# A static order by lag and list, and a static order by one turn number per piece, for a fused attention and recurrence kernel

## The chip, the cores and the metric

The kernel runs on one core of a Trainium2 chip. The core has five engines that run side by side, each through its own list of instructions in the order in which the list was written: TensorE (PE, matmuls), VectorE (DVE), ScalarE (ACT), GpSimd (POOL) and SyncE (SP, which here issues every DMA). An instruction may wait for semaphores; what stands behind it on the same engine waits with it. The metric is the time of one execution in microseconds. Timed runs of the kernel before gave a median of 693.77 us (3 runs, 692.63 to 694.01).

## The reference

For each of 16 sequences of 128 tokens with 256 channels, in float32:

```
# block L0, on x[b] and the context ctx[b]
x = x + attention(layernorm(x), mask of the first kind) @ w_ao      # 16 heads of 16
x = x + attention(layernorm(x), keys and values from ctx, mask[b]) @ w_co
x = x + gelu(layernorm(x) @ w1) @ w2                                # 4 * 256 hidden
# block L1, a recurrence over the 128 tokens, with first states from ctx[b]
xn = layernorm(x); five mixed streams of xn and its shifted difference
w = exp(-exp(decay)); r, k, v, g = projections of the streams       # 32 heads of 8
s_t = k_t v_t + w_t s_(t-1);  out_t = r_t (u k_t v_t + s_(t-1))
x = x + (groupnorm(out) * silu(g)) @ Wo
x = x + sigmoid(xr @ Wr) * (square(relu(xk @ Wk)) @ Wv)             # xk, xr mixed as above
```

In the attention, `scores = scores * mask - 10000 * (1 - mask)` comes before the softmax. The sequences do not depend on each other.

## The kernel before, in words

**Pieces.** The work on one sequence b (called item b below) is cut into small functions, "pieces", each with one engine. Their first letter names the stage: `a_` is the attention (second argument 0 for the self attention, 1 for the cross attention; a pair such as `(0, 2)` is the attention and a group of four heads), `b_` is the MLP and the preparation of the recurrence, `d_` is the recurrence and all after it. Each engine has 80 to 1408 pieces in all. Those that matter below:

- `a_scale` on ACT (line 1231, `A_LT<-PS_S`) turns a normalised x, transposed by PE (`a_turn`), into the layer's input. `a_val`, `a_key`, `a_query` on PE wait for it, and the scores wait for those.
- `a_lessmask` on ACT (line 1272, `MADD<-MASK`) makes `10000 * mask[b] - 10000` for the cross attention of item b. For b = 0 it waits for `in_rest`, the semaphore of two DMAs from line 473 (all cross masks) and line 474 (x of items 1 to 15). In later items it does not wait for a DMA.
- `a_exps` on ACT are the exponentials, `a_prob_turn`, `a_pv` and `a_out` on PE the rest of the attention.
- `b_decay2`, `b_decays` on ACT make the decays (`DW` line 1356, `EW` line 1362), which SP spreads over 8 rows with a DMA (`b_wspread`). `b_keyrec` (`KR`, line 1350) and `b_values` (`VC`, line 1370) move keys, receptances and values out of PSUM; PE's `b_valgate` writes into the same PSUM bank that `b_keyrec` of ACT empties and so waits for it. `b_gatetanh` is `TG` (line 1375).
- `d_outer` (AJ), `d_scan` (SS, line 1057) on DVE are the recurrence. In the last two items the values are spread by PE (`b_select`, line 767).
- `d_root_of` on ACT (line 1407, a square root, and for item 14 a short `Tanh` behind it at line 1410) and DVE's `d_inverse`, `d_norm` are the group norm in the last two items; the other items do it with Newton steps on DVE. `d_yturn` (PE, `PS_D<-CST,O`), `d_affine` (ACT, line 1431), `d_gated` (DVE, `YT`), `d_out` (PE, line 559 `PS_D<-W,YT`), `d_sum` (DVE, line 1166) follow each other.
- `b_shift` (SX, line 1520) and `d_shift` (SM, line 1531) on POOL take differences of two SBUF tensors.

**Order.** The order of an engine's list is written out by hand: a table per engine (`PE_ORDER` and so on) with rows (piece, argument, lag). The program goes through steps i = 0, 1, ..., and in each step through the table; the row issues its piece for item i - lag, where such an item exists. So all items have the same order inside a step, those at the start and the end included; up to seven items are in work at once. No piece is left out and none is issued twice. `KEEP_WARM` adds matmuls on the identity in front of some PE pieces of the first and the last items.

**ACT tables.** Some functions of ACT need another table than the one that is loaded (`ACT_TABLE_LOAD` in the list); the compiler puts a load wherever the function that follows asks for another table, so their number depends on the order.

Its wait for the DMAs:

```
def a_lessmask(b, _):
    if not later(b):                       # later(b) is b > 0
        act.wait_ge(in_rest, IN_REST)
```

Of the kernel before, what the change touches and what calls it, by code (L numbers as in the profile page):

```python
# [88 lines left out]
PE_ORDER = [
    ("a_prob_turn", (1, 0), 3), ("d_own", 0, 5), ("a_prob_turn", (1, 1), 3), ("b_low2", 2, 4), ("d_read", 0, 5),  # L90
    ("a_prob_turn", (1, 2), 3), ("b_decay1", 0, 4), ("d_oturn", 0, 5), ("a_enc_turn", 0, 2),
    ("a_prob_turn", (1, 3), 3), ("b_decay2", 0, 4), ("b_keyrec", 0, 4), ("b_keyrec", 1, 4), ("a_val", 1, 2),
    ("a_pv", 1, 3), ("a_turn", 1, 2), ("b_valgate", 0, 4), ("b_valgate", 1, 4), ("a_key", 1, 2), ("a_out", 1, 3),
    ("a_query", 1, 2), ("d_biasout", 0, 5), ("d_yturn", 0, 5), ("a_prob_turn", (0, 0), 1), ("a_scores", 1, 2), ("a_prob_turn", (0, 1), 1),
    ("b_select", 0, 4), ("b_turn", 0, 3), ("d_out", 0, 5), ("a_turn", 0, 0), ("b_mlp1", 0, 3), ("b_mlp1", 1, 3),
    ("b_mlp2", 0, 3), ("a_prob_turn", (0, 2), 1), ("d_turn", 0, 5), ("b_mlp2", 1, 3), ("a_val", 0, 0),
    ("a_key", 0, 0), ("b_select", 1, 4), ("a_prob_turn", (0, 3), 1), ("a_query", 0, 0), ("a_pv", 0, 1),
    ("b_turn", 1, 3), ("d_keyrec", 0, 5), ("d_keyrec", 1, 5), ("a_out", 0, 1), ("b_low1", 0, 3), ("d_val", 0, 5),
    ("a_scores", 0, 0), ("b_low2", 0, 3)]
DVE_ORDER = [  # L100
    ("a_mask", (0, 1), 1), ("b_streams", 0, 4), ("a_prob_copy", (1, 1), 3), ("d_own", 0, 5),
    ("a_addmask", (0, 1), 1), ("b_streams", 1, 4), ("a_inverse", 1, 3), ("b_streams", 2, 4), ("a_maxima", (0, 0), 1),
    ("d_output", 0, 5), ("a_prob_copy", (1, 3), 3), ("d_means", 0, 5), ("d_centre", 0, 5), ("a_mask", (0, 2), 1),
    ("a_normal", 1, 2), ("d_spread", 0, 5), ("d_guess", 0, 5), ("a_mask", (0, 3), 1), ("d_guess", 1, 5),
    ("d_guess", 2, 5), ("a_maxima", (0, 1), 1), ("d_newton", (0, 0), 5), ("d_newton", (0, 1), 5),
    ("d_newton", (0, 2), 5), ("d_newton", (1, 0), 5), ("d_newton", (1, 1), 5), ("a_stats", 0, 0),
    ("d_newton", (1, 2), 5), ("a_moments", 0, 0), ("d_newton", (2, 0), 5), ("a_context", 1, 3),
    ("d_newton", (2, 1), 5), ("a_maxima", (0, 2), 1), ("a_addmask", (0, 3), 1), ("a_key", 1, 2),
    ("d_newton", (2, 2), 5), ("a_normal", 0, 0), ("d_inverse", 0, 5), ("d_norm", 0, 5), ("d_ruk", 0, 4), ("a_sum", 1, 3),
    ("b_stats", 0, 3), ("b_moments", 0, 3), ("a_query", 1, 2), ("a_maxima", (0, 3), 1), ("d_gated", 0, 5),  # L110
    ("b_normal", 0, 3), ("b_gate", 0, 4), ("a_mask", (1, 0), 2), ("a_mask", (1, 1), 2), ("a_mask", (1, 2), 2),
    ("d_sum", 0, 5), ("a_prob_copy", (0, 1), 1), ("a_mask", (1, 3), 2), ("d_stats", 0, 5), ("a_maxima", (1, 0), 2),
    ("a_addmask", (1, 3), 2), ("d_moments", 0, 5), ("a_maxima", (1, 1), 2), ("a_maxima", (1, 2), 2),
    ("d_outer", 0, 4), ("d_normal", 0, 5), ("d_scan", 0, 4), ("b_sum", 0, 3), ("b_stats", 1, 3),
    ("a_prob_copy", (0, 3), 1), ("a_inverse", 0, 1), ("a_key", 0, 0), ("b_moments", 1, 3), ("d_shift", 0, 5), ("d_mixed", 0, 5),
    ("a_maxima", (1, 3), 2), ("b_normal", 1, 3), ("d_rstate", 0, 4), ("d_mixed", 1, 5), ("d_outer", 1, 4),
    ("a_context", 0, 1), ("a_query", 0, 0), ("b_mixed", 0, 3), ("d_scan", 1, 4), ("d_relu2", 0, 5), ("d_mixing", 0, 5), ("d_final", 0, 5), ("a_sum", 0, 1),
    ("a_stats", 1, 1), ("a_mask", (0, 0), 0), ("a_moments", 1, 1), ("d_rstate", 1, 4)]
ACT_ORDER = [
    ("a_exps", (1, 0, 0), 3), ("a_prob_copy", (0, 3), 2), ("a_key", (0, 0), 1), ("a_widen", 0, 2),  # L120
    ("a_exps", (1, 0, 1), 3), ("a_spread", 0, 2), ("b_scale", 1, 4), ("a_exps", (1, 1, 0), 3), ("a_val", 0, 1),
    ("d_keyrec", 0, 6), ("d_relu2", 0, 6), ("a_key", (0, 1), 1), ("b_low", 0, 4), ("a_exps", (1, 1, 1), 3),
    ("a_exps", (1, 2, 0), 3), ("a_exps", (1, 2, 1), 3), ("a_prob_copy", (1, 0), 3), ("d_first_states", 0, 4),
# [11 lines left out]
    ("a_root", 1, 2), ("a_addmask", (0, 2), 1), ("a_addbias", 0, 1), ("a_root", 0, 0), ("a_addbias", 1, 2),  # L135
    ("b_root", 0, 3), ("b_addbias", 0, 3), ("a_addmask", (1, 0), 2), ("a_addmask", (1, 1), 2),
    ("a_addmask", (1, 2), 2), ("d_gates", 0, 5), ("d_root", 0, 5), ("d_shift", 0, 5), ("b_root", 1, 3), ("b_shift", 0, 3),
    ("d_rstate", 0, 4)]

LAG = max(lag for order in (SP_ORDER, PE_ORDER, DVE_ORDER, ACT_ORDER, POOL_ORDER) for _, _, lag in order)  # L140

# [1495 lines left out]
```

## Time and profile before

| what | value |
| --- | --- |
| timed runs, median | 693.77 us |
| profiled execution, span from first to last instruction | 694.0 us |
| PE busy | 645.3 us, 93% |
| DVE busy | 598.2 us, 86% |
| ACT busy | 571.7 us, 82% |
| POOL busy | 311.6 us, 45% |
| DMA | 50.44 MB, mean 73 GB/s |
| chain that ended last | PE 80%, DVE 8%, ACT 7% |

The span of the profiled execution is 0.2 us over the median of the timed runs and inside their spread; there is nothing around the span that has to be added. The page of the profile gives, in 40 slices of 17.35 us, the busy share of each engine in tenths. The views by window give the busy time of each engine in a stretch; the timelines give single instructions with their start, their length, and in brackets how long the engine had been idle and what ended that.

### The profile page before, as it was taken

What the parts mean: (1) busy time and instruction counts of PE and PEld (TensorE: products, weight loads), DVE (VectorE), ACT (ScalarE), POOL (GpSimd) and SP (SyncE); (2) the same over time, 40 slices, a digit from 0 to 9 for tenths busy, and PEclk for the clock granted to TensorE, in tenths of its full rate; (3) what the DMA queues carried; (4) which work ended last, traced back from release to release, by engine and by line L of the source; (5) the groups of instructions that cost most, each with busy time, mean ns of one, the idle gap of its engine ahead of it and who ended that gap; (6) DMA issues with size and microseconds to landing.
All of it is one profiled execution on the core that took longest, in us unless ns stands there. A gap on an engine that the chain in (4) does not pass through costs nothing.

```text
span 694.0 us, 17297 instructions
## 1 busy us (share of the span) xinstructions
PE 645.3 (93%) x5877; PEld 561.6 (81%) x5877; DVE 598.2 (86%) x1430; ACT 571.7 (82%) x2071; POOL 311.6 (45%) x440
## 2 busy tenths in 40 slices
PE   6878998999999999999999999999999989898776
PEld 5666787888989888988989888989888877687555
DVE  3598588999999999999999999999999987968274
ACT  1568899899999999999999999999999987664513
POOL 1154252646464554636364646454554624432120
PEclk9999999999999999999999999999999999999799
DMA  8920031221305050504122231305050503120200
GB/s 306 325 70 9 2 104 36 70 70 58 88 9 138 1 146 1 145 2 122 25 85 62 67 81 53 93 4 144 1 146 1 146 0 108 31 70 0 69 9 8
DMA packets 53725, 50.44 MB, mean 73 GB/s; under 512 B 6030, under 2 KB 48902, under 8 KB 53254
## 3 DMA queue, kind: packets, MB, share of 16 engines
q1 hardware_dynamic: 53638, 49.34, 24.7%
q8 instruction: 47, 0.77, 0.5%
q14 instruction: 40, 0.33, 0.1%
HBM read 28.62 MB, written 3.93 MB: 47 GB/s over the span
## 4 chain that ended last, share of the span: by engine, by line
PE 80%; DVE 8%; ACT 7%; issue 3%; POOL 1%; DMA 0%; SPq 0%; DVEq 0%; ACTq 0%; POOLq 0%
PE PS_B L552 16%; PE PS_T L654 9%; PE PS_B L694 8%; PE PS_S L552 7%; PE PS_D L559 5%; PE PS_S L625 4%; PE PS_T L662 4%; PE PS_S L559 4%; PE PS_T L559 4%; ACT SC L1291 3%; PE PS_D L800 2%; PE PS_B L703 2%; PE PS_D L552 2%; ACT PT L1301 2%; PE PS_T L545 2%
## 5 line engine op out<-in xcount | busy, mean ns | idle before, releaser
L1291 ACT ACTIVATE SC<-SC,NMX 128x128 f32<-128x128 f32 x512 | 200.0, 398 | 0.2
L1291 ACT ACTIVATION_READ_ACCUMULATOR SC<-SC,NMX 128x1 f32 x512 | 101.0, 197 | 0.0
L654 PE MATMUL PS_T<-CST,SC 128*128 128x128 f32 x512 | 81.3, 281 | 7.7 <-ACT PT L1301 3.6
L976 DVE TENSOR_REDUCE NMX<-SC 128x4 f32<-128x512 f32 x128 | 85.2, 676 | 0.4 <-POOL SC L1499 0.3
L1301 ACT ACTIVATE PT<-PS_T 128x512 f32<-128x512 f32 x120 | 70.8, 590 | 12.7 <-PE PS_T L654 12.7
L654 PEld LDWEIGHTS PS_T<-CST,SC 128*128 128x128 f32 x512 | 56.4, 141 | 26.1 <-ACT PT L1301 12.7
L1057 DVE TENSOR_TENSOR_SCAN SS<-W,AJ 128x1024 f32<-128x1024 f32 x32 | 73.2, 2288 | 0.2
L552 PE MATMUL PS_B<-MX,W 128*128 128x128 f32 x512 | 64.2, 280 | 4.7 <-ACT KR L1350 4.7
L552 PEld LDWEIGHTS PS_B<-MX,W 128*128 128x128 f32 x512 | 61.3, 196 | 4.9 <-ACT KR L1350 4.9
L1499 POOL TENSOR_TENSOR SC<-SC,MADD 128x512 f32<-128x512 f32 x48 | 59.9, 1276 | 6.5 <-DVE SC L956 6.5
L552 PE MATMUL PS_B<-B_LT,W 128*128 128x128 f32 x512 | 61.1, 278 | 1.0 <-ACT B_LT L1231 0.9
L694 PE MATMUL PS_B<-W,HG 128*128 128x256 f32 x256 | 61.9, 385 | 0.0
L552 PEld LDWEIGHTS PS_B<-B_LT,W 128*128 128x128 f32 x512 | 58.4, 192 | 3.2 <-ACT B_LT L1231 1.9
L1501 POOL TENSOR_TENSOR SC<-SC,MADD 128x512 f32<-128x512 f32 x32 | 42.2, 1318 | 40.4 <-DVE SC L956 40.4
L956 DVE TENSOR_TENSOR SC<-PS_S,MASK 128x512 f32<-128x512 f32 x80 | 51.9, 683 | 4.0 <-PE PS_S L625 4.0
L552 PE MATMUL PS_S<-A_LT,W 128*128 128x128 f32 x384 | 51.8, 280 | 1.3 <-DVE SC L967 1.3
L552 PEld LDWEIGHTS PS_S<-A_LT,W 128*128 128x128 f32 x384 | 50.3, 196 | 3.1 <-DVE SC L967 1.5
L1544 POOL TENSOR_TENSOR SS<-SS,KR 128x1024 f32<-128x1024 f32 x14 | 33.1, 2363 | 41.0 <-DVE SS L1057 41.0
L694 PEld LDWEIGHTS PS_B<-W,HG 128*128 128x128 f32 x256 | 46.1, 190 | 5.6
L1536 POOL TENSOR_TENSOR MX<-MX,XN 128x256 f32<-128x256 f32 x80 | 48.4, 634 | 3.1 <-DVE MX L1029 2.9
L1262 ACT ACTIVATE KP<-PS_S,KB,CST 128x128 f32<-128x128 f32 x112 | 46.1, 480 | 0.8 <-PE PS_S L552 0.8
L1029 DVE SCALAR_TENSOR_TENSOR MX<-PS_B,COL,SX 128x128 f32<-128x128 f32 x160 | 44.1, 336 | 0.7 <-PE PS_B L716 0.7
(231 smaller groups left out, 1595.0 us busy)
## 6 DMA issues: line engine op xcount, KB each, us to landing
W<-EW SPq DMA_DIRECT2D x32, 512.0 KB, 4.1
...
```

The source lines that it names most:

```text
L552: last = pe.matmul(dst[:, m * T:(m + 1) * T], w(name, kt, n, lo + m * P, lo + (m + 1) * P), rhs[:, kt, 0:T], start=(kt == 0), stop=(kt == ...
L559: last = pe.matmul(dst, lhs[:, kt, 0:T], w(name, kt, n, lo, lo + C), start=(kt == 0), stop=(kt == CT - 1))
L654: last = pe.transpose(PS_T[:, j * T:(j + 1) * T], SC[:, nr(b, a) % 2, g, j, :], ident)
L694: last = pe.matmul(PS_B[:, 1, 0:C], HG[:, kt, :], w("w2", kt, C, 0, C), start=(kt == 0), stop=(kt == FT - 1))
L956: dve.tensor_tensor(masked, PS_S[:, g], over_heads(mask), ALU.mult).then_inc(a_masked, 1)
L976: dve.tensor_reduce(NMX[:, nr(b, a) % 2, GH * g:GH * g + GH], SC[:, nr(b, a) % 2, g], AX_X, ALU.max, negate=True)\
L1057: dve.tensor_tensor_scan(SS[:, t].rearrange("p d n -> p (d n)"), W8[:, t].rearrange("p d n -> p (d n)"), AJ[:, t].rearrange("p d n -> p (d ...
L1262: last = act.activation(KP[:, par, t, :], keys[:, t * T:(t + 1) * T], ACT.Identity, bias=KB[:, a, par, t:t + 1], scale=CST[:, K_PAR + par: ...
L1291: last = act.activation(SC[:, nr(b, a) % 2, g, j, :], SC[:, nr(b, a) % 2, g, j, :], ACT.Exp, bias=NMX[:, nr(b, a) % 2, h:h + 1], accum_out ...
L1301: act.activation(PT[:, g], PS_T[:, :].rearrange("p (j n) -> p j n", n=T), ACT.Copy)\
L1499: pool.tensor_tensor(SC[:, nr(b, a) % 2, g], SC[:, nr(b, a) % 2, g], over_heads(MADD[:, b % 2, :]), ALU.add).then_inc(a_added, 1)
L1536: last = pool.tensor_tensor(MX[:, i], MX[:, i], XN[:, :, 1:T + 1], ALU.add)
```

## The change

Each row of a table now holds a turn number instead of a lag, and a second table per engine (`..._MOVED`) holds other turn numbers for single items. A piece of item b has the place `10000 * b + turn`, and an engine's pieces are issued in the order of these places. The instructions of the pieces, their semaphores and their waits are as before, and so is `KEEP_WARM`. The set of pieces on each engine is the same: 80 on SP, 800 on PE, 1408 on DVE, 944 on ACT, 336 on POOL.

```diff
+TURN = 10000
+
 SP_ORDER = [
-    ("b_vspread", 0, 4), ("d_store", 0, 6), ("b_wspread", 0, 3), ("b_vstore", 0, 3), ("a_load", 0, 0)]
+    ("a_load", 0, 90000), ("b_wspread", 0, 110004), ("b_vstore", 0, 110008), ("b_vspread", 0, 120002),
+    ("d_store", 0, 170026),
+]
...
+ACT_MOVED = {
+    ("a_scale", 0): {0: -49998, 2: 9934, 4: 8789, 12: 7950}, ("a_key", (0, 0)): {4: 10734, 15: 10413},
...
+    ("a_lessmask", 0): {0: -50000, 1: -59996, 5: 17742, 10: 27746, 12: 25187, 13: 22838},
...
+def in_order(order, moved):
+
+    turns = [(TURN * b + moved.get((name, arg), {}).get(b, turn), name, arg, b)
+             for name, arg, turn in order for b in range(B)]
+    return [(name, arg, b) for _, name, arg, b in sorted(turns, key=lambda t: t[0])]
...
-        def run(pieces, order, i):
-
-            for name, arg, lag in order:
-                if 0 <= i - lag < B:
-                    pieces[name](i - lag, arg)
+        def run(pieces, order, moved):
+
+            for name, arg, b in in_order(order, moved):
+                pieces[name](b, arg)
...
-            for i in range(B + LAG):
-                run(pieces, ACT_ORDER, i)
+            run(pieces, ACT_ORDER, ACT_MOVED)
```

The file is 153 lines longer ahead of the pieces, so line 1272 of before is line 1425 of the change, 1231 is 1384, and so on. What moves is shown at three places.

**The first instructions of ACT.** `A_LT` is `a_scale` of item 0, `VP` its `a_val`, `MADD` is `a_lessmask`; in brackets stand the semaphores waited for. Before:

```order
L1224 ACTIVATE EARLY<-EW 128x1 [waits set_dve]
L1231 ACTIVATE A_LT<-PS_S,COL 128x128 [waits a_lnps,set_dve,in_first]
L1231 ACTIVATE A_LT<-PS_S,COL 128x128
L1253 ACTIVATE VP<-PS_S 128x8x16 [waits a_pvps,a_vps]
L1253 ACTIVATE VP<-PS_S 128x8x16
```

The same place in the change:

```order
L1377 ACTIVATE EARLY<-EW 128x1 [waits set_dve]
L1425 ACTIVATE MADD<-MASK 128x128 [waits in_rest,set_dve,in_first]
L1384 ACTIVATE A_LT<-PS_S,COL 128x128 [waits a_lnps]
L1384 ACTIVATE A_LT<-PS_S,COL 128x128
L1425 ACTIVATE MADD<-MASK 128x128
L1406 ACTIVATE VP<-PS_S 128x8x16 [waits a_pvps,a_vps]
```

`a_lessmask` of item 0, with its wait for `in_rest`, now stands ahead of `a_scale` of item 0, and that of item 1 behind it. Before, the one of item 0 was the 23rd piece of ACT.

**ACT in the last two items.** `DW`, `EW`, `KR`, `VC`, `TG` belong to item 15, `OQ`, `GE` and `PS_D<-PS_D,GNC` to the group norm of item 14. Before:

```order
L1356 ACTIVATE DW<-PS_B,COL 128x128 x2
L1401 ACTIVATE OQ<-O 128x256
L1407 ACT_TABLE_LOAD
L1407 ACTIVATE GE<-PS_D,EPST 128x32
L1410 ACT_TABLE_LOAD
L1410 ACTIVATE EARLY<-EW 128x1
L1362 ACTIVATE EW<-DW 128x2x127
L1364 ACT_TABLE_LOAD
L1364 ACTIVATE EARLY<-EW 128x1
L1350 ACTIVATE KR<-PS_B 128x512
L1370 ACTIVATE VC<-PS_B 128x256
L1375 ACT_TABLE_LOAD
```

The same place in the change:

```order
L1509 ACTIVATE DW<-PS_B,COL 128x128 x2
L1515 ACTIVATE EW<-DW 128x2x127
L1517 ACT_TABLE_LOAD
L1517 ACTIVATE EARLY<-EW 128x1
L1503 ACTIVATE KR<-PS_B 128x512
L1560 ACTIVATE GE<-PS_D,EPST 128x32
L1563 ACT_TABLE_LOAD
L1563 ACTIVATE EARLY<-EW 128x1
L1584 ACTIVATE PS_D<-PS_D,GNC 128x128 x2
L1528 ACTIVATE TG<-PS_B 128x256
L1523 ACTIVATE VC<-PS_B 128x256
```

`EW` and `KR` of item 15 now stand ahead of the square root of item 14, and the stretch holds two table loads instead of four.

**PE in the last two items.** `PS_B<-MX,W` are the key, receptance, value and gate matmuls of item 15 (four pieces of four), `PS_D<-CST,O` is `d_yturn`, `PS_D<-W,YT` `d_out` of item 14, `PS_S<-VC,SEL` `b_select` of item 15. Before:

```order
L746 MATMUL PS_B<-DT,W 128x128 x2
L552 MATMUL PS_B<-MX,W 128x128 x16
L545 MATMUL PS_D<-CST,O 128x128 x2
L767 MATMUL PS_S<-VC,SEL 128x128 x8
L541 MATMUL PS_T<-CST 128x128 x2
L559 MATMUL PS_D<-W,YT 128x256 x2
```

The same place in the change:

```order
L901 MATMUL PS_B<-DT,W 128x128 x2
L707 MATMUL PS_B<-MX,W 128x128 x12
L700 MATMUL PS_D<-CST,O 128x128 x2
L707 MATMUL PS_B<-MX,W 128x128 x4
L696 MATMUL PS_T<-CST 128x128 x2
L714 MATMUL PS_D<-W,YT 128x256 x2
L922 MATMUL PS_S<-VC,SEL 128x128 x8
```

`d_yturn` of item 14 went ahead of the last four of the sixteen, and `b_select` of item 15 behind `d_out` of item 14.

## Rows read from the trace of the kernel before

**Rows 1.** The page, 40 slices: busy tenths of PE, then its granted clock.
```profile
PE   6878998999999999999999999999999989898776
PEclk9999999999999999999999999999999999999799
```

**Rows 2.** Busy us by window: window, length, PE, PEld, DVE, ACT, POOL, clock, DMA.
```profile
0.00:40.00 40.00, 28.95 (x205) 23.76 (x205) 21.74 (x55) 15.82 (x63) 10.49 (x19) 1.00 0.88 303
40.00:160.00 120.00, 108.85 (x1027) 93.15 (x1026) 100.33 (x221) 106.56 (x404) 52.19 (x75) 1.00 0.15 42
160.00:560.00 400.00, 398.70 (x3805) 353.00 (x3804) 385.93 (x949) 379.96 (x1395) 211.05 (x291) 1.00 0.26 70
560.00:640.00 80.00, 71.40 (x606) 60.46 (x605) 62.71 (x149) 51.74 (x176) 30.19 (x43) 0.96 0.16 46
640.00:694.00 54.00, 37.44 (x240) 31.21 (x240) 27.48 (x60) 17.63 (x38) 7.72 (x14) 0.87 0.09 27
```

**Rows 3.** Timeline of ACT, first 38 us: start, length, instruction, idle before and its end.
```profile
8.27 0.81 ACT L1231 ACTIVATE A_LT<-PS_S,COL 128x128 f32<-128x128 f32 x2 [6.03 <-PE PS_S L545]
...
32.14 0.32 ACT L1272 ACTIVATE MADD<-MASK 128x128 f32<-128x128 f32 x1
37.30 0.17 ACT L1241 ACTIVATE PREV<-PS_S 128x4 f32<-128x4 f32 x1 [4.83 <-PE PS_S L545]
```

**Rows 4.** Timeline of SP, the DMA of x for items 1 to 15.
```profile
5.74 6.40 SPq L474 DMA_DIRECT2D X<-in_x  x1
```

**Rows 5.** Timeline of DVE, first 36 us: what waited for that DMA.
```profile
21.51 0.43 DVE L890 BATCH_NORM_STATS2 A_ST<-X 128x6 f32<-128x256 f32 x1 [1.02 <-DMA X<-in_x]
```

**Rows 6.** Timeline of PE, first 36 us: the first matmuls on `A_LT`.
```profile
9.13 2.08 PE L559 MATMUL PS_S<-W,A_LT 128*128 128x256 f32 x4
11.00 3.19 PE L552 MATMUL PS_S<-A_LT,W 128*128 128x128 f32 x16
```

**Rows 7.** Timeline of ACT, 645 to 660 us.
```profile
646.24 0.62 ACT L1356 ACTIVATE DW<-PS_B,COL 128x128 f32<-128x128 f32 x2 [0.80 <-PE PS_B L746]
...
647.28 1.28 ACT L1407 ACT_TABLE_LOAD   x1
648.58 0.29 ACT L1407 ACTIVATE GE<-PS_D,EPST 128x32 f32<-128x32 f32 x1
648.88 1.28 ACT L1410 ACT_TABLE_LOAD   x1
650.18 0.20 ACT L1410 ACTIVATE EARLY<-EW 128x1 f32<-128x1 f32 x1
650.29 0.40 ACT L1362 ACTIVATE EW<-DW 128x254 f32<-128x254 f32 x1
...
652.11 0.58 ACT L1350 ACTIVATE KR<-PS_B 128x512 f32<-128x512 f32 x1
...
658.53 0.77 ACT L1431 ACTIVATE PS_D<-PS_D,GNC 128x128 f32<-128x128 f32 x2
```

**Rows 8.** Timeline of PE, 640 to 662 us.
```profile
642.03 1.94 PE L800 MATMUL PS_D<-SS,HS 128*32 128x256 f32 x16
...
652.74 3.78 PE L552 MATMUL PS_B<-MX,W 128*128 128x128 f32 x16 [4.75 <-ACT KR L1350]
...
660.13 1.03 PE L559 MATMUL PS_D<-W,YT 128*128 128x256 f32 x4
```

**Rows 9.** Timeline of DVE, 638 to 694 us.
```profile
649.29 0.42 DVE L1148 TENSOR_TENSOR O<-O,PS_D 128x256 f32<-128x256 f32 x1
...
661.19 0.42 DVE L1166 TENSOR_TENSOR X<-PS_D,X 128x256 f32<-128x256 f32 x1 [0.98 <-PE PS_D L559]
...
663.74 2.29 DVE L1057 TENSOR_TENSOR_SCAN SS<-W,AJ 128x1024 f32<-128x1024 f32 x1
```

**Rows 10.** All instructions of POOL's line 1520: length in ns, least, median, most.
```profile
L1520 POOL TENSOR_TENSOR SX<-XN x16: 612/612/1749, 83.4 to 634.7; 128x256 f32<-128x256 f32 x16
```

**Rows 11.** Timeline of POOL, 584 to 640 us.
```profile
601.64 1.75 POOL L1520 TENSOR_TENSOR SX<-XN 128x256 f32<-128x256 f32 x1 [2.01 <-ACT XN L1231]
```

**Rows 12.** Timeline of DVE, the same stretch.
```profile
601.70 1.22 DVE L1050 TENSOR_TENSOR AJ<-V,KR 128x1016 f32<-128x1016 f32 x1
```

More of the change, by code:

```diff
@@ L84 @@
     ('d_keyrec', 0, 15): 4, ('d_val', 0, 15): 2}
+TURN = 10000
 SP_ORDER = [
-    ("b_vspread", 0, 4), ("d_store", 0, 6), ("b_wspread", 0, 3), ("b_vstore", 0, 3), ("a_load", 0, 0)]
-PE_ORDER = [
[L90 to L99, printed above, removed]
@@ L100 @@
-DVE_ORDER = [
[L101 to L118, printed above, removed]
@@ L133 @@
-POOL_ORDER = [
-    ("d_final", 0, 6), ("a_addmask", (0, 0), 1), ("b_addnorm", 0, 4), ("b_addnorm", 1, 4), ("b_addnorm", 2, 4),
[L135 to L140, printed above, removed]
+    ("a_load", 0, 90000), ("b_wspread", 0, 110004), ("b_vstore", 0, 110008), ("b_vspread", 0, 120002),
@@ new lines @@
+    ("d_store", 0, 170026),
+]
+SP_MOVED = {
+    ("b_wspread", 0): {11: 120002, 12: 110008, 13: 110006}, ("b_vstore", 0): {2: 110002, 11: 120004, 12: 120002},
+    ("b_vspread", 0): {1: 110012, 11: 120006, 12: 120004},
+}
+PE_ORDER = [
+    ("a_turn", 0, 5845), ("a_val", 0, 7312), ("a_key", 0, 7410), ("a_query", 0, 7959), ("a_scores", 0, 9566),
+    ("a_prob_turn", (0, 0), 14631), ("a_prob_turn", (0, 1), 15131), ("a_prob_turn", (0, 2), 16323),
+    ("a_prob_turn", (0, 3), 17781), ("a_pv", 0, 18202), ("a_out", 0, 19031), ("a_enc_turn", 0, 21631),
+    ("a_val", 1, 22442), ("a_turn", 1, 22844), ("a_key", 1, 22853), ("a_query", 1, 24031), ("a_scores", 1, 24831),
+    ("a_prob_turn", (1, 0), 30031), ("a_prob_turn", (1, 1), 30431), ("a_prob_turn", (1, 2), 30972),
+    ("a_prob_turn", (1, 3), 31868), ("a_pv", 1, 32831), ("a_out", 1, 33632), ("b_turn", 0, 35637),
+    ("b_mlp1", 0, 36078), ("b_mlp1", 1, 36150), ("b_mlp2", 0, 36409), ("b_mlp2", 1, 36882), ("b_turn", 1, 38500),
+    ("b_low1", 0, 39300), ("b_low2", 0, 39900), ("b_low2", 2, 40700), ("b_decay1", 0, 41287), ("b_decay2", 0, 42100),
+    ("b_keyrec", 0, 42362), ("b_keyrec", 1, 42500), ("b_valgate", 0, 42974), ("b_valgate", 1, 43267),
+    ("b_select", 0, 45545), ("b_select", 1, 47695), ("d_own", 0, 50300), ("d_read", 0, 50900), ("d_oturn", 0, 51479),
+    ("d_biasout", 0, 54337), ("d_yturn", 0, 54513), ("d_out", 0, 55700), ("d_turn", 0, 56793), ("d_keyrec", 0, 58705),
+    ("d_keyrec", 1, 58900), ("d_val", 0, 59500),
+]
@@ L519, in _ @@
             pieces = named(a_load, b_vstore, b_vspread, b_wspread, d_store)
-            for i in range(B + LAG):
-                run(pieces, SP_ORDER, i)
+            run(pieces, SP_ORDER, SP_MOVED)
             sp.wait_ge(stored, 16 * B)
@@ L864, in _ @@
                            d_own, d_read, d_oturn, d_yturn, d_biasout, d_out, d_turn, d_keyrec, d_val)
-            for i in range(B + LAG):
-                run(pieces, PE_ORDER, i)
+            run(pieces, PE_ORDER, PE_MOVED)
         @block.vector
@@ L1216, in _ @@
                            d_moments, d_mixed, d_mixing)
-            for i in range(B + LAG):
-                run(pieces, DVE_ORDER, i)
+            run(pieces, DVE_ORDER, DVE_MOVED)
         @block.scalar
@@ L1569, in _ @@
                            d_rstate, d_gates, d_root)
-            for i in range(B + LAG):
-                run(pieces, POOL_ORDER, i)
+            run(pieces, POOL_ORDER, POOL_MOVED)
 def kernel(**inputs):
```

183 lines of the change are left out of this document (169 added, 14 removed), and 3 rows, old and new, of the table PE_MOVED.

## Prediction, on record before the change was run

> **What bounds the kernel now.** I read the page first. Its 40 slices [rows 1] show PE at 9 tenths in all slices from the eighth to about the thirty-second, and lower at both ends. The same in windows [rows 2]: from 160 to 560 us PE is busy for 398.70 of 400 us, DVE for 385.93 and ACT for 379.96, at the full granted clock. Here no order can gain more than the 1.3 us in which PE is idle, because the PE instructions are the same. What an order can gain or lose lies at the ends: PE is idle for 11.05 us from 0 to 40, 11.15 us from 40 to 160, 8.60 us from 560 to 640 and 16.56 us from 640 to 694 [rows 2]. So I looked at both ends in the timelines, engine by engine, and held the new order against them. Two places carry nearly the whole sum, and they have opposite signs.
>
> **The start: a wait moved to the head of ACT.** Before, ACT's first work on data is `a_scale` of item 0, which starts at 8.27 us, when PE has turned the normalised x [rows 3]. Everything follows from it: PE's value, key and query matmuls at 9.13 and 11.00 us [rows 6], then the scores, the masks and the exponentials. In the change `a_lessmask` of item 0 stands ahead of it, and it waits for `in_rest`. The second DMA of that semaphore is issued at 5.74 us [rows 4] as the tenth of a row. When it lands is shown by DVE: it sat idle 1.02 us for this very DMA and went on at 21.51 us [rows 5]. ACT does this instruction only at 32.14 us before [rows 3], when the data had long been there, and so pays nothing.
>
> In the change ACT starts it at about 21.5 us. The instruction is 0.32 us long [rows 3]; the next one may start some 0.1 us before its end. So `a_scale` starts at 21.5 + 0.2 = 21.7 us instead of 8.27, which is 13.4 us later. Queued behind it on ACT is everything that ACT does. PE's next piece, `a_val` of item 0, waits for `a_scale`; DVE's next, `a_key` and `a_query` of item 0, wait for PE; POOL's next, the first mask sum, waits for DVE. There is nothing of another item ahead of them on any engine, so nothing hides the 13.4 us. SP goes on with its loads, but none of these is waited for before 13.4 us later except the one here: the 1.02 us that DVE idles for x of item 1 falls away, yet ACT was busy with exponentials then, and I count nothing for it. The `a_lessmask` of item 1 (0.32 us) lies behind `a_scale`, where ACT waits for PE's value matmuls of 2.08 us [rows 6]: nothing. These four records of 2.08 us take 1.03 us at 660.13 [rows 8]: twice as long, so they run at the lower of the clock's two levels (1.2 of 2.4 GHz), although the window's mean reads 1.00. In the change PE has again been idle before them, and I let the same matmuls take the same time. Bounds of this term: below 12.0 us, if the DMA lands earlier by the spread that one landing may have (a tenth of its 15.8 us from issue to the start at 21.51); above 15.5 us, if as much half clock comes again behind these matmuls as they show (2.08 and 3.19 us in [rows 6] are together some 2 us over the full clock). I take 13.4.
>
> **The end: two table loads less.** From 640 us few pieces are left and one chain runs through all engines. Before, between the decays and `KR` of item 15 ACT does the square root of item 14's group norm, with a table load before it and one behind [rows 7]: 1.28 + 0.29 + 1.28 + 0.20, from 647.28 to 650.29, are 3.0 us. PE sits idle 4.75 us for `KR` at the end of it [rows 8]. In the change `EW`, a load and `KR` come first, then the root. With DW ending as before, `KR` starts at 652.11 - 3.0 = 649.1 and ends at 649.7.
>
> From there I follow item 14, since the recurrence of item 15 on DVE stands behind its sum. The root (0.29) is done at 650.0; DVE's reciprocal and `d_norm` (before 0.7 us from the root's end at 648.87 to the end of `O` at 649.71 [rows 7, 9], so 0.8) at 650.8. PE has done the first four value matmuls by then, and `d_yturn` stands right behind them and no longer behind all of 3.78 us [rows 8]: about 651.2. ACT has loaded its table by 650.0 + 1.28 + 0.20 = 651.5, which is later, so `d_affine` starts at 651.5. Before, it started at 658.53 [rows 7]. That is 7.0 us. In front of DW, in the matmuls of item 14's read-out and item 15's streams, the new order puts `d_own`, `d_read` and `d_oturn` together, and the record of 1.94 us in [rows 8] lies in a half-clock stretch; here I estimate 1.5 us, from nothing (no gain) to 3 us (the 1.94 us halved, and `d_oturn` before two matmul groups). What is late next: from `d_affine` the chain goes on over `d_out` and the sum at 661.19 to the scan at 663.74 [rows 8, 9], in the same steps. `b_select` of item 15 is now behind `d_out`, but the scan's first multiplication waits for item 14's sum and its statistics on DVE anyway (661.19 to 662.3), which is about as long as four of the eight matmul pairs. The row of the decays that SP spreads starts 3 us earlier too. Sum of the end: 7.0 + 1.5 = 8.5 us earlier. Bounds: 3.0, if only the path to `KR` shortens and the rest waits for something else; 11, with the 3 us in front and 1 us of the clock.
>
> **Meetings on the shared port.** POOL's line 1520, two SBUF tensors of 256 elements, takes 612 ns in the median and 1749 ns at most [rows 10]. The long one is at 601.64 us, beside DVE's multiplication of two SBUF tensors from 601.70 to 602.92 [rows 11, 12], and DVE waited for it after. The 16 executions have a median equal to the minimum, so in the steady part there is no such meeting in this line to be taken away. I take 1.14 us (1749 - 612) for the one on the path, and bound it by 0 and 2.
>
> The Trainium skill (SBUF — State Buffer, section "SBUF: two separate sides") says that VectorE, with two SBUF inputs, and GpSimd take an exclusive lock on a shared port pair for the whole instruction and that the loser is fully blocked. The trace agrees: the two instructions of rows 11 and 12 show 1749 against 612 ns. By this rule the change's numbers could also make new meetings wherever they shift one list against the other, and then the term would be zero or a loss; that it would be a gain in the steady part the rule does not give, with no meeting in line 1520 there.
>
> **The start after the first waits (40 to 160 us).** The PE idle of 11.15 us is made of many waits below 1.5 us; ACT has the longest, 4.83 us, at 37.30 [rows 3]. In the change the query and scores of item 1 stand ahead of item 0's `a_out`, which brings item 1's exponentials forward and item 0's cross attention back. My value is 1.0 us gained. The trace doesn't show the new order, so the bounds are wide: a gain of half the idle time, 5.6 us, or a loss of 2 us. The orders of the stores on SP cost nothing: nobody waits for `d_store` but the end, and the last one is last in both.
>
> **The sum.** Against the profiled execution's span: 694.0 + 13.4 - 8.5 - 1.1 - 1.0 = 696.8 us. The span is 0.2 us over the median of the timed runs, nothing is added around it, and I forecast 697.
>
> **Rivals.**
>
> 1. *The ends give back more than the start costs* (faster). Half of the idle time from 40 to 160 us, 5.6 us, and half of the 8.60 us from 560 to 640, 4.3 us, would go instead of the 2.1 us above: 694.0 + 13.4 - 8.5 - 9.9 = 689.0. It is decided at 40 to 160 us, from the point where more than 4.9 us go beside the 8.5. For it: these stretches do have single items moved in their own tables. Against it: ACT is already busy for 106.56 of the 120 us [rows 2], so there is little room in which to bring work forward. 0.14.
> 2. *Loss and gain cancel.* The end gives its bound of 11 us and the fill 3: 694.0 + 13.4 - 11.0 - 3.0 = 693.4. 0.18.
> 3. *The end does not shorten beyond `KR`.* The scan of item 15 is then held by its own inputs (the spread values behind `d_out`, or a half-clock stretch such as that of rows 8): 694.0 + 13.4 - 3.0 - 1.0 = 703.4. For it: in the last 54 us the mean granted clock is 0.87 [rows 2], and any idle gap can bring it about. 0.14.
> 4. *The steady part loses its cover.* DVE is busy for 96.5% there and ACT for 95.0% [rows 2]; many pieces of both change places in every item. If PE idles 0.5 us more per sequence, over ten sequences that is 5 us: 701.8. Against it: two lists that are merely permuted within their slack leave PE as it is. 0.08.
> 5. *The wait at the head costs nothing*, so the change does what it says without a price: 694.0 - 8.5 - 2.1 = 683.4. It needs `in_rest` to be there at 8.3 us, and rows 4 and 5 say 21.5. 0.04.
>
> The forecast, 696.8 with 695.3 to 700 as its own range, has 0.42.
>
> **How the numbers follow.** 0.2% of the time is 1.4 us, about what a measurement of this kernel can tell from no change. Faster (below 692.4) are rivals 1 and 5 and a little of 2: 0.19. Within it lie most of rival 2 and a little of the forecast's lower side: 0.18. The rest, 0.63, is slower. For 8 in 10 the range leaves out rival 5, half of rival 1 and a little of rival 3: 689.5 to 703.5.
>
> **What would show it.** In the profile of the change, ACT's `MADD<-MASK` is the first instruction after the early exponential, with an idle time of over 18 us that a DMA ends, and `A_LT<-PS_S` starts at 21.7 us. If it starts before 12 us, the main term is wrong. The time between that start and the end of the steady part must be about as before; PE's idle time from 50 to 175 us tells the fill. At the end, `KR` of item 15 has one table load before it, PE's wait for it is below 3 us, and from `A_LT` of item 0 to the last instruction pass 675 us instead of 685.7. A steady part with PE busy below 99% would speak for rival 4. From the start of `KR` to that of item 15's first scan pass 11.6 us before [rows 7, 9]; my sum makes them 656.7 - 649.1 = 7.6, and if they stay above 10, rival 3 is right.

## The result

| | median | runs |
| --- | --- | --- |
| before | 693.89 us | 4, from 692.63 to 694.44 |
| changed | 699.16 us | 4, from 697.62 to 700.14 |

The ratio is 1.0081, with a 95% interval from 1.006 to 1.0102: the change made the kernel slower by about 5.3 us. 697 had been forecast, with a range from 689.5 to 703.5. The sign and the two large terms were right. One term was 3 us too small and another of 3 us was missing; they have opposite signs, and so the sum did not show them.

### The profile page after: what moved, and what is told of

Read it like the earlier page. It is cut to its first block, busy times and chain, and to the rows that moved or that the text cites. A ratio compares the mean times of both kernels' runs of the same rounds, so it can differ in the third digit from the quotient of the medians.

```text
span 697.2 us, 17295 instructions
## 1 busy us (share of the span) xinstructions
PE 640.5 (92%) x5877; PEld 559.4 (80%) x5877; DVE 602.1 (86%) x1430; ACT 569.8 (82%) x2069; POOL 311.1 (45%) x440
## 4 chain that ended last, share of the span: by engine, by line
PE 68%; DVE 12%; ACT 10%; issue 5%; DMA 2%; POOL 1%; SPq 1%; DVEq 0%; POOLq 0%; ACTq 0%
PE PS_B L707 13%; PE PS_B L849 7%; PE PS_T L809 7%; PE PS_S L707 6%; PE PS_D L714 5%; PE PS_T L817 4%; PE PS_S L780 3%; PE PS_S L714 3%; ACT SC L1444 3%; PE PS_T L714 2%; DMA X<-in_x 2%; PE PS_D L955 2%; ACT PT L1454 2%; PE PS_D L707 2%; PE PS_T L700 2%
## 5 line engine op out<-in xcount | busy, mean ns | idle before, releaser
L1444 ACT ACTIVATION_READ_ACCUMULATOR SC<-SC,NMX 128x1 f32 x512 | 103.9, 203 | 0.0
L849 PE MATMUL PS_B<-W,HG 128*128 128x256 f32 x256 | 59.4, 379 | 0.0
```

The source lines that it names most:

```text
L849: last = pe.matmul(PS_B[:, 1, 0:C], HG[:, kt, :], w("w2", kt, C, 0, C), start=(kt == 0), stop=(kt == FT - 1))
L1444: last = act.activation(SC[:, nr(b, a) % 2, g, j, :], SC[:, nr(b, a) % 2, g, j, :], ACT.Exp, bias=NMX[:, nr(b, a) % 2, h:h + 1], accum_out ...
```

## The profile after

The page of the changed kernel: busy tenths of PE in 40 slices of 17.4 us, then its granted clock.

```profile
PE   2578999999999999999999999999999989989776
PEclk9999999999999999999999999999999999999999
```

Against [rows 1] the first slices of PE are at 2, 5 and 7 where 6, 8 and 7 stood, the dip to 8 in the seventh slice and the clock's slice at 7 near the end are gone. In windows (columns as in [rows 2]):

```profile
0.00:40.00 40.00, 17.29 (x99) 14.59 (x99) 12.23 (x33) 9.73 (x38) 6.59 (x14) 1.00 0.87 299
40.00:160.00 120.00, 110.99 (x1038) 94.27 (x1039) 98.88 (x226) 102.89 (x390) 53.65 (x75) 0.99 0.16 43
160.00:560.00 400.00, 396.69 (x3803) 351.33 (x3802) 388.02 (x941) 378.06 (x1398) 207.94 (x287) 1.00 0.24 66
640.00:697.20 57.20, 42.84 (x319) 36.59 (x317) 37.45 (x75) 20.70 (x53) 10.30 (x18) 1.00 0.11 35
```

PE has 11.66 us less work done at 40 us than before (28.95 - 17.29). From 160 to 560 us it idles 3.31 us where it had idled 1.30. At the end the clock is 1.00 where it was 0.87. From 40 to 160 us it is 0.99 instead of 1.00: the window from 40 to 80 us has 0.96 in the change and 1.00 before.

The start, timeline of ACT (start, length, instruction, in brackets the idle time before it and what ended it):

```profile
2.04 0.20 ACT L1377 ACTIVATE EARLY<-EW 128x1 f32<-128x1 f32 x1
21.99 0.31 ACT L1425 ACTIVATE MADD<-MASK 128x128 f32<-128x128 f32 x1 [19.75 <-DMA X<-in_x]
22.20 0.79 ACT L1384 ACTIVATE A_LT<-PS_S,COL 128x128 f32<-128x128 f32 x2
```

and of PE and DVE behind it:

```profile
23.05 2.07 PE L714 MATMUL PS_S<-W,A_LT 128*128 128x256 f32 x4 [14.27 <-ACT A_LT L1384]
```

```profile
26.87 1.37 DVE L1089 TENSOR_SCALAR KP<-PS_S,CST,KB 128x128 f32<-128x128 f32 x4 [19.68 <-PE PS_S L707]
```

`A_LT` starts at 22.20 instead of 8.27 us [rows 3]. All three engines stand still for the same DMA.

The end, timeline of ACT (it answers to [rows 7]), then PE (to [rows 8]):

```profile
657.62 0.62 ACT L1509 ACTIVATE DW<-PS_B,COL 128x128 f32<-128x128 f32 x2 [0.28 <-PE PS_B L901]
658.27 0.41 ACT L1515 ACTIVATE EW<-DW 128x254 f32<-128x254 f32 x1
658.71 1.28 ACT L1517 ACT_TABLE_LOAD   x1
660.00 0.20 ACT L1517 ACTIVATE EARLY<-EW 128x1 f32<-128x1 f32 x1
660.11 0.58 ACT L1503 ACTIVATE KR<-PS_B 128x512 f32<-128x512 f32 x1
660.59 0.28 ACT L1560 ACTIVATE GE<-PS_D,EPST 128x32 f32<-128x32 f32 x1
660.88 1.28 ACT L1563 ACT_TABLE_LOAD   x1
662.18 0.20 ACT L1563 ACTIVATE EARLY<-EW 128x1 f32<-128x1 f32 x1
662.29 0.76 ACT L1584 ACTIVATE PS_D<-PS_D,GNC 128x128 f32<-128x128 f32 x2
```

```profile
653.18 1.07 PE L955 MATMUL PS_D<-SS,HS 128*32 128x256 f32 x16
...
660.74 1.16 PE L707 MATMUL PS_B<-MX,W 128*128 128x128 f32 x8 [1.28 <-ACT KR L1503]
661.77 0.44 PE L700 MATMUL PS_D<-CST,O 128*128 128x128 f32 x2
662.04 1.06 PE L707 MATMUL PS_B<-MX,W 128*128 128x128 f32 x8
```

`KR` has one table load before it, PE waits 1.28 us for it instead of 4.75, and the same 16 value matmuls take 1.16 + 1.06 us instead of 3.78.

The steady part, 14 executions of DVE's line 1271 (line 1117 before), lengths in ns: least, median, most. The prediction had no term for this row; before it reads 172/172/181.

```profile
L1271 DVE TENSOR_SCALAR GT<-GE x14: 163/360/1277, 143.1 to 628.6; 128x32 int32<-128x32 int32 x14
```

One of the long ones on DVE, and what POOL did at that time:

```profile
366.50 1.26 DVE L1271 TENSOR_SCALAR GT<-GE 128x32 int32<-128x32 int32 x1
```

```profile
366.45 1.27 POOL L1653 TENSOR_TENSOR SC<-SC,MADD 128x512 f32<-128x512 f32 x1
```

**Where the time went.** The same piece in both traces, at points along the program (starts; "scan" is DVE's scan of the recurrence, line 1057 before and 1211 after):

| point | before | after | offset | step |
| --- | --- | --- | --- | --- |
| `A_LT` of item 0 | 8.27 | 22.20 | +13.9 | start +13.9 |
| first scan of item 3 | 222.93 | 232.94 | +10.0 | fill -3.9 |
| first scan of item 13 | 595.26 | 608.32 | +13.1 | steady +3.1 |
| `DW` of item 15 | 646.24 | 657.62 | +11.4 | |
| `KR` of item 15 | 652.11 | 660.11 | +8.0 | |
| `d_affine` of item 14 | 658.53 | 662.29 | +3.8 | |
| first scan of item 15 | 663.74 | 668.07 | +4.3 | |
| last instruction | 694.0 | 697.2 | +3.2 | end -9.9 |

## Experiments

In each set "before" was run along, and a ratio is against it. Several kernels join the two orders. They hold the lists of before beside the new ones and use one helper; the order of a stretch is told by the list and the piece at which it ends:

```diff
+def by_lag(order):
+    return [(name, arg, i - lag) for i in range(B + LAG) for name, arg, lag in order if 0 <= i - lag < B]
+def spliced(*parts):
+    done = []
+    for order, upto in parts:
+        left = [p for p in order if p not in done]
+        done += left[:left.index(upto)] if upto else left
+    return done
```

### The start: the wait taken out of the change, and put into before

```diff
-    ("a_lessmask", 0): {0: -50000, 1: -59996, 5: 17742, 10: 27746, 12: 25187, 13: 22838},
+    ("a_lessmask", 0): {5: 17742, 10: 27746, 12: 25187, 13: 22838},
```

> The changed kernel with one edit: a_lessmask of items 0 and 1 back at the turn that ACT's order gives to all other items (behind item 0's a_spread), everything else as in the change. The changed kernel took 699.2 us, before 693.9. Theory A (the wait at the head delays everything by what A_LT of item 0 showed, 22.20 - 8.27 = 13.9 us, and the order behind it is good for its own sake): 699.2 - 13.9 = 685.3 us. Rival B (of the 4 us that the fill gave back, from an offset of 13.9 to 9.8 us, all was slack that a late start swallows, and comes back as idle time when the start is early): 685.3 + 4.0 = 689.3 us. Rival C (the start is not what sets the time): about 699.

Measured: 684.28 us, before 694.58, ratio 0.9858 (0.9833 to 0.9884). Theory A, within about 1 us: the two pieces cost 14.9 us, of which `A_LT` shows 13.9. The trace of the changed kernel also has a window at a lower clock (0.96 from 40 to 80 us), and this one has none there (1.00); that fits the missing microsecond, but no run isolates it.

```diff
+            pieces["a_lessmask"](0, 0)
+            at = next(k for k, p in enumerate(ACT_ORDER) if p[0] == "a_lessmask")
             for i in range(B + LAG):
-                run(pieces, ACT_ORDER, i)
+                run(pieces, ACT_ORDER[:at], i)
+                if i >= ACT_ORDER[at][2] + 1:
+                    run(pieces, ACT_ORDER[at:at + 1], i)
+                run(pieces, ACT_ORDER[at + 1:], i)
```

> The kernel before with one edit: a_lessmask of item 0 stands at the head of ACT's work, everything else in the order of before. This is the start term alone. Theory A: 693.9 + 13.9 = 707.8 us, A_LT of item 0 at about 22.2 us. Rival B (the late start is partly swallowed in the fill whatever the order): 703.9 us, with an offset of the sums against before that falls from 13.9 to about 9.8 us by 160 us. Rival C (wait costs nothing): 693.9.

Measured: 708.91 us, ratio 1.0219 (1.0193 to 1.0245), 14.3 us more than before; theory A. Timeline of its ACT:

```profile
21.76 0.31 ACT L1272 ACTIVATE MADD<-MASK 128x128 f32<-128x128 f32 x1 [19.52 <-DMA X<-in_x]
21.98 0.79 ACT L1231 ACTIVATE A_LT<-PS_S,COL 128x128 f32<-128x128 f32 x2
```

The offset is 13.7 us at `A_LT` and still 13.7 at item 3's scan (236.63 against 222.93). So nothing in the fill swallows a late start. With the new order and the early start the same scan stands at 217.75, 5.2 us ahead of before. The fill's gain is thus the order's own, and not a rebound; it is 3.9 us in the changed kernel's trace and 5.2 us here, without the stretch at the lower clock.

### The steady part, put back at item 5 and at item 8

```diff
-            run(pieces, PE_ORDER, PE_MOVED)
+            run(pieces, spliced((in_order(PE_ORDER, PE_MOVED), ('a_val', 0, 5)),
+                                (by_lag(OLD_PE), ('b_turn', 0, 15)), (in_order(PE_ORDER, PE_MOVED), None)))
```

and the same on DVE, ACT and POOL.

> The changed kernel with the order of before on PE, DVE, ACT and POOL from the first piece of item 5 up to the third block's entry (b stage) of item 15; fill, end and SP stay as changed. In the changed kernel the offset of its sums against before grew from 9.8 to 13.1 us in this stretch, and PE's windows showed 0.3 to 0.5 us idle per 40 us where before had 0.1. Theory D (this is the steady order's doing, the mechanism of rival 4 of the prediction at two thirds of its size): 699.2 - 3.3 = 695.9 us, an offset that stays near 10 us, and PE busy over 99.6% from 240 to 560 us. Rival E (it comes from something else that runs along, such as the stores on SP or the clock): 699.2 us.

Measured: 697.54 us, ratio 1.0062 (1.0036 to 1.0088). This is between D and E, and the trace tells why: the offset is flat, as D says (15.0 us at item 7's scan, 15.1 at item 12's), but it had risen from 11.3 to 14.9 within two items of the switch. Item 5's own pieces are among those that the new lists move (`a_val` of item 5 by 1049 on PE), so the switch probably jumbles the join; the trace shows only that the loss lies there. The second run:

> The same base (684.3 us), with all four engines in the order of before from item 8 (not 5) up to the b stage of item 15. The switch at item 5 gave a flat offset behind it, but cost 5 us of the fill's gain within two items. Theory K (that was the price of a switch inside the fill; at item 8, in the steady part, it is small, and the later growth of 3.2 us goes): 681.5 us. Rival L (the order of before needs more distance between the engines; the 4 to 5 us that the fill gave back are lost wherever one switches): 686 us or more, with PE's idle time in the two items behind the switch.

The edit is the same with 8 for 5, on the kernel with `a_lessmask` back at its turn. Measured: **680.01 us**, ratio 0.9805 (0.9781 to 0.9829), the best of all. Theory K. The offset is -3.9 at item 3's scan and -3.8 at item 12's, and in the windows (columns as in [rows 2]), first the changed kernel, then this one:

```profile
300.00:540.00 240.00, 237.50 (x2246) 210.15 (x2246) 233.44 (x555) 227.01 (x827) 123.86 (x172) 1.00 0.25 68
```

```profile
300.00:540.00 240.00, 239.19 (x2307) 211.35 (x2299) 231.76 (x571) 227.84 (x845) 127.88 (x176) 1.00 0.24 65
```

### Which engine's steady order

Base: the changed kernel with `a_lessmask` back at its turn. The edit is the one above, at 5, on the engines named.

> The changed kernel with a_lessmask back at its turn (684.3 us), and DVE alone in the order of before from item 5 up to the b stage of item 15. Its offset against before grew by 3.2 us in the steady part (from -5.3 to -2.1), and the waits that PE had there were for DVE's QT and CTX. Theory D1 (DVE's new steady order makes that loss): 681.1 us, PE busy over 99.6% from 240 to 560 us. Rival D2 (it is PE's own or ACT's): 684.3 us or more, the growth of the offset unchanged.

Measured: 695.92 us, ratio 1.0022 (1.0006 to 1.0039).

> The same base (684.3 us), with PE and ACT in the order of before from item 5 up to the b stage of item 15, DVE and POOL as changed. Theory D2 (PE's or ACT's steady order makes the 3.2 us loss): 681.1 us. Theory D1 (DVE's): 684.3 us. Rival J (the orders fit only each other; a mixture loses more than either): 687 us or more.

Measured: 687.56 us, ratio 0.9904 (0.9883 to 0.9925). The times speak for rival J in both. The offsets say more: with PE and ACT put back it still rises in the same steps as in the change, from -0.9 (item 3's scan) to +2.0 (item 12's), 2.9 us against 3.2. So PE's and ACT's new order isn't needed for the loss. With DVE alone put back, it rises by 11.6 us: a mixture that fits nobody.

```diff
+DVE_MOVED = {piece: {b: turn for b, turn in at.items() if not 6 <= b <= 13} for piece, at in DVE_MOVED.items()}
```

> The changed kernel with a_lessmask back at its turn (684.3 us), and with DVE's single exceptions (DVE_MOVED) left out for items 6 to 13, so that DVE repeats one pattern there; PE, ACT and POOL keep theirs. Theory N1 (the steps at items 8, 9, 11 and 13 come from DVE's single exceptions): 681.5 us, a flat offset near -5.3 us. Rival N2 (they come from the regular part of DVE's order, or the exceptions fit those of PE and ACT and taking them out costs more): 684.3 us or more.

Measured: 690.44 us, ratio 0.9948 (0.9927 to 0.9969), 6.2 us worse than its base; rival N2. The offset rises from -5.3 us (item 3's scan) to +1.1 (item 12's), 6.5 us, where it rises by 3.2 us with the exceptions: they save half of it. And DVE's new order from item 8 on, alone in the kernel before:

```diff
-            for i in range(B + LAG):
-                run(pieces, DVE_ORDER, i)
+            run(pieces, spliced((by_lag(OLD_DVE), ('a_stats', 0, 8)),
+                                (in_order(DVE_ORDER, DVE_MOVED), ('b_stats', 0, 15)), (by_lag(OLD_DVE), None)))
```

> The kernel before with the changed order on DVE alone, from item 8 up to the b stage of item 15; PE, ACT, POOL and SP as before throughout. With PE and ACT back in the order of before the offset still rose in the same steps at items 8, 9, 11 and 13, by 2.8 us; with all four back it stayed flat. Theory M1 (DVE's order alone makes PE wait there): 693.9 + 2.8 = 696.7 us, a rising offset and PE busy for less than 99.4% from 300 to 540 us. Rival M2 (POOL's order, which was left as changed in both, or DVE's only together with another's): 693.9 us and a flat offset.

Measured: 695.14 us, before 694.31, ratio 1.0017 (1.0002 to 1.0031): 0.8 us, under a third of M1's price. In the trace the offset rises by 2.2 us from item 3's scan to item 12's, most of what M1 said; why so little of it is left in the time, no run shows.

**What the runs have in common.** `GT<-GE` is a shift of 32 integers per partition, SBUF to SBUF, one of the steps of the group norm's root on DVE. The rows of its 14 executions in the kernels with a flat offset (the wait at the head of before; the 680 us kernel):

```profile
L1117 DVE TENSOR_SCALAR GT<-GE x14: 172/172/182, 146.7 to 628.8; 128x32 int32<-128x32 int32 x14
```

```profile
L1343 DVE TENSOR_SCALAR GT<-GE x14: 165/172/656, 129.0 to 609.9; 128x32 int32<-128x32 int32 x14
```

and where it rises (PE and ACT put back; DVE without exceptions; DVE's order alone):

```profile
L1343 DVE TENSOR_SCALAR GT<-GE x14: 181/364/1276, 129.1 to 616.6; 128x32 int32<-128x32 int32 x14
```

```profile
L1273 DVE TENSOR_SCALAR GT<-GE x14: 163/336/1273, 127.8 to 617.1; 128x32 int32<-128x32 int32 x14
```

```profile
L1343 DVE TENSOR_SCALAR GT<-GE x14: 169/358/490, 131.9 to 614.5; 128x32 int32<-128x32 int32 x14
```

In the changed kernel four of these instructions took over 1 us: at 328.93, 366.50, 442.51 and 517.75 us (group norms of items 5, 6, 8 and 10), each ending with the POOL mask sum (`SC<-SC,MADD`, 1.27 to 1.29 us, of items 9, 10, 12 and 14) that had started ahead of it. Of the 4.9 us of DVE's time that they took (1.08 + 1.26 + 1.28 + 1.27), some 4.2 are over the 172 ns of before; the offset rose by 3.1 to 3.2. Its steps fall between the sums on either side of the same four. On the kernel with the early start the meetings are at 313.74, 351.33, 427.33 and 502.57 us, and the offset of DVE's residual sums (line 1152, before 998) steps like this:

| meeting | sum ahead of it | sum behind it | step |
| --- | --- | --- | --- |
| 313.74 | 303.8: -5.69 | 320.0: -4.75 | 0.94 |
| 351.33 | 341.9: -4.86 | 358.0: -3.99 | 0.87 |
| 427.33 | 417.4: -3.71 | 433.5: -2.86 | 0.85 |
| 502.57 | 492.6: -2.97 | 508.3: -2.45 | 0.52 |

The four steps make 3.18 us, the whole rise of 3.2. In the run with PE and ACT put back the steps at its four meetings are nearly the same: 0.94, 0.87, 0.87 and 0.52 us.

In the run of DVE's order alone `GT<-GE` has no long meeting, but DVE meets GpSimd on other lines. `RK<-KR` is a product of two SBUF tensors and takes 418 to 425 ns in all 16 executions of before; `A_N` is a normalised x, 0.41 us alone:

```profile
L1293 DVE TENSOR_TENSOR RK<-KR x16: 391/417/923, 98.2 to 651.0; 128x256 f32<-128x256 f32 x16
```

```profile
542.37 1.27 DVE L1136 TENSOR_SCALAR A_N<-X,A_MV,A_RS 128x256 f32<-128x256 f32 x1
```

The two long `RK<-KR` stand at 358.34 and 433.23 us beside a GpSimd addition of 0.73 us, the long `A_N` beside a mask sum of 1.28 us. They lost 0.50, 0.51 and 0.86 us. The offset of the residual sums steps by 0.46, 0.47 and 0.83 us across them, 1.76 of the 1.84 us that it rises from 249 to 549 us. PE waits 0.33 us for DVE's `QT` some 4.4 us behind each of the two `RK<-KR`, as it does 8 us behind the first three meetings of the kernel with the early start. Not every meeting costs: in the same run `SS<-SS,KR` takes 1.67 instead of 1.22 us four times beside `SM<-XM`, and the offset does not step there. With DVE alone put back, the run that lost most, `GT<-GE` takes 0.88 to 1.01 us four times and POOL's `SX<-XN` 1242 ns in the median instead of 612.

So meetings of DVE with GpSimd that the order of before does not have are the likely cause of the steady loss: time, place and size agree in three traces, on three different lines. It is not isolated: no run took these meetings away and left the rest of the order, and what else the orders change on DVE ahead of `QT` is not excluded.

### The end

The new order of the end on PE, DVE, ACT and POOL in the kernel before:

```diff
+            run(pieces, spliced((by_lag(OLD_ACT), ('b_scale', 0, 15)), (in_order(ACT_ORDER, ACT_MOVED), None)))
```

> The kernel before with the changed kernel's order only at the end: on PE, DVE, ACT and POOL from the b stage of item 15 on; SP as before. Theory F (the end gives back alone what the spans showed, 13.1 - 3.2 = 9.9 us, mostly because KR comes before the root of item 14's group norm and d_affine starts early): 693.9 - 9.9 = 684.0 us, KR of item 15 to its first scan about 8.0 us instead of 11.6. Rival G (part of the gain stems from the order of item 14 ahead of this cut): 693.9 - 7.0 = 686.9 us or more. Rival H (only the two table loads less, the 3.0 us on KR): 690.9 us.

Measured: 683.84 us, ratio 0.9861 (0.9834 to 0.9887). Theory F. Then one piece on ACT alone:

```diff
+            order = [(name, arg, i - lag) for i in range(B + LAG) for name, arg, lag in ACT_ORDER if 0 <= i - lag < B]
+            order.remove(("d_root_of", 0, 14))
+            order.insert(order.index(("b_keyrec", 0, 15)) + 1, ("d_root_of", 0, 14))
...
```

> The kernel before with one piece moved on ACT alone: the root of item 14's group norm (d_root_of) goes behind KR of item 15 (b_keyrec) instead of ahead of the decays; two table loads less. PE, DVE, POOL, SP as before. The whole tail order brought 694.6 to 683.8, and its profile had 3.4 us of half clock where the one of before had 20. Theory F1 (ACT's move is the main part and brings d_affine 7 us forward, since PE can do d_yturn as soon as KR has let it through the value matmuls): 694.6 - 7 = 687.6 us or less. Theory F2 (it brings only the 3.0 us on the way to KR; the rest needs d_yturn and d_out ahead of other matmuls on PE): 691.6 us. Theory F3 (F2 and, PE being idle for less long ahead of the value matmuls, the half clock of 6.8 us behind them goes as well, which gives some 3 us more): 688.6 us.

Measured: 687.3 us, before 693.75, ratio 0.9903 (0.9885 to 0.9921). By time F1, by mechanism F3 as well. Its PE:

```profile
639.95 1.94 PE L800 MATMUL PS_D<-SS,HS 128*32 128x256 f32 x16
...
647.53 2.05 PE L552 MATMUL PS_B<-MX,W 128*128 128x128 f32 x16 [1.63 <-ACT KR L1350]
...
650.05 2.05 PE L767 MATMUL PS_S<-VC,SEL 128*128 128x128 f32 x16 [0.26 <-ACT VC L1370]
```

The wait is 3.12 us shorter than in [rows 8], two table loads of 1.28 us and the work beside them; and the 16 value matmuls behind it take 2.05 instead of 3.78 us, at 2.4 instead of 1.2 GHz. The complement:

> The kernel before with the changed order at the end (from the b stage of item 15) on PE, DVE and POOL, and ACT as before throughout: the complement of the run that moved one piece on ACT alone, which took 687.3 us. The whole tail order took 683.8 us. Theory Q1 (the parts add up: 694.2 - 10.8 + 6.7 = 690 us): the 2 us ahead of the decays come, and 1 to 2 us behind KR, but KR still stands behind two table loads more and PE's long wait for it. Theory Q2 (PE's order gives nothing without ACT's, since d_affine stays behind b_values on ACT): 692 us, only the part ahead of the decays. Theory Q3 (it makes things worse, since PE's second half of the value matmuls now waits for ACT's late d_affine path): 695 us or more.

Measured: 695.27 us, before 694.31, ratio 1.0018 (1.0004 to 1.0031). Q3's size and nearly Q2's mechanism; the additive Q1 is out by 5 us. Its PE:

```profile
651.24 2.03 PE L779 MATMUL PS_B<-MX,W 128*128 128x128 f32 x8 [4.56 <-ACT KR L1575]
...
658.44 2.07 PE L786 MATMUL PS_D<-W,YT 128*128 128x256 f32 x4 [2.85 <-DVE YT L1387]
```

PE's new order waits 2.85 us at `d_out` for `d_affine`, which ACT still does last, and the clock is at its lower level again behind the waits (4 matmuls in 2.07 us). ACT's one move is worth 6.5 us, the other three engines' order alone nothing or a small loss, and the whole end 10.7. The whole holds more than these two: ACT's other moves at the end (such as `d_affine` of item 14 ahead of `TG` and `VC` of item 15) are in neither part. So the 4 to 5 us that are left over come from the interplay with PE, from ACT's other moves, or from both; no run puts ACT's whole new end alone into before.

### The fill: is it made in the first two items?

The 680 us kernel with the switch at item 2 (`a_turn`, `a_stats`, `a_scale`, `a_root` of item 2) instead of item 8.

> The kernel that took 680.0 us (the changed kernel with a_lessmask back at its turn and the order of before from item 8 to the b stage of item 15), with the switch to the order of before at item 2 instead of item 8: the changed order stands only in the pieces of items 0 and 1 ahead of item 2's first piece, and at the end. Of the fill's gain of 5.3 us the offsets showed 4.3 at KR of item 0. Theory R1 (the gain is made in the first two items and keeps): 680 us. Theory R2 (it is built up by many small moves over items 0 to 4, and what the first two bring is lost at the switch, as at item 5): 684 us, the time with the changed tail alone. Between: 682 us.

Measured: 687.79 us, before 694.62, ratio 0.9901 (0.9875 to 0.9927). R2, and 4 us worse than it said. The offset is +1.7 us already at the first scan of item 0 and +2.2 in item 12. So the changed order of items 0 and 1 alone does not bring the gain. Whether the gain is made only in later items, or made early and lost at the switch as at item 5, this run cannot tell. The gain is kept where the changed order stands up to item 8. In its profile one stretch of half clock lies at 27.5 us, as at 26.5 us in the 680 us kernel's, so that is no difference between the two.

## Why the prediction was right, and where it was wrong

- **The start, 13.4 us: right.** 13.9 in the trace, 14.3 in the time with this edit alone in before. `A_LT` started at 22.20 (21.7 forecast); DVE's 19.68 us and PE's 14.27 us of idle time are the queue behind the wait. Rival 5 (no cost) is refuted. The matmuls behind the wait stayed at half speed, as assumed (2.07 us against 2.08 in [rows 6]).
- **The end, -8.5 us: right in mechanism, 1.4 too small.** In front of `DW` -1.7 (forecast -1.5), `DW` to `KR` -3.4 (-3.0), `KR` to `d_affine` -4.2 (-4.0, the 7.0 less the 3.0), then +0.5 and -1.1. From the start of `KR` to the first scan pass 7.96 us; 7.6 were forecast and 11.6 was before. Rival 3 is refuted. Its reason, that any idle gap can bring the half clock about, is too wide: in the change PE idles 1.97 us ahead of the matmuls at 672.42 us, and they ran at the higher level. What the sum named only as a bound of 1 us, the clock, is in these numbers: 3.78 us of matmuls became 2.22 and 1.94 became 1.07, together 2.4 us. Behind the first scan of item 15 these and the next group took 1.16 and 1.03 us where before had 1.34 and 1.92: 1.1 us, as much as the last step. So up to 3.5 of the 9.9 us are the clock's. A slip without effect: from the root's end to the end of `O` pass 0.84 us, not 0.7; the sum used 0.8.
- **The fill, -1.0 us: mis-sized.** It gave 3.9, within the bounds (-5.6 to +2). I chose the value near nothing because ACT was busy for 106.56 of 120 us. But ACT's share did not bound it: with the early start PE is busy for 113.54 us of this window and ACT for 111.18. ACT's idle time of 4.83 us, which I named as the longest wait of this window, ends at 37.30 us and so lies ahead of it. Rival 1 had this mechanism at 5.6 us.
- **The steady part, nothing: wrong.** It cost 3.1 us. This is rival 4, to which I gave 0.08 at 5 us. The step that failed is its "against": two lists that are merely permuted within their slack leave PE as it is. With the order of before put back from item 8 on, the offset stays flat (-3.9 to -3.8 us) and the time falls from 684.3 to 680.0 us. My own sign for it, PE busy below 99%, was too coarse as well: 396.69 of 400 us is 99.2%, and 3 us are lost all the same.
- **Meetings on the port, -1.1 us: wrong sign.** I priced the one meeting that before shows and that the order may take away. In the change it is shorter (1749 ns before, at most 1097 now, in item 15 instead of 14). But the new order made four meetings of over 1 us on `GT<-GE`, which before has none. The prediction quoted the Trainium skill (SBUF — State Buffer, section "SBUF: two separate sides") that the loser of the shared port pair is fully blocked, and said that the new numbers could make meetings as well; it did not follow this up. In the traces `GT<-GE` is held for as long as the rule says (1.26 us beside POOL's 1.27, against 172 ns). But the prediction quoted the rule for two SBUF inputs only, and `GT<-GE` has one; the same section also counts a VectorE instruction in a 2-port mode, and no run here shows which mode this one is in. The term should have been a loss: 4.2 us of DVE's time in the four meetings, and probably the steady part's 3.1 us.
- **The frame: wrong by 1.8 us.** I wrote, ahead of the prediction and in it, that the span of the profiled execution stands 0.2 us over the median and that nothing is added around it. But every execution listed since has its time 1.7 to 1.9 us above its span (699.04 and 697.2 for the changed kernel). The profiled execution of before thus took 695.8 us, some 1.9 more than the median of its timed runs. Its span's mean clock was 0.985. Among 15 later executions of before the three at 0.993 took 690.7 to 691.3 us and the three at 0.983 took 696.0 to 696.2. So I compared the span of a sample at the long end of this spread with the others' times, and the 1.8 us around the span hid it. By spans the change costs 3.2 us (my sum: 2.8), by timed medians 5.3.

The forecast of 697 is 2.2 us below the result: 0.4 us of the sum by spans, and the 1.8 us around the span. That the sum itself is so close is luck: the fill's 2.9 us and the steady part's 3.1 us nearly cancel, and so do the end's 1.4 us and the 1.1 us of the meeting. A reader should not take the closeness for proof of each term.
